# Second attention: where the mask, the ranks' comparison and the read of the flags stand in VectorE's queue

## The chip, the cores and the metric

The kernel runs on one core of a Trainium2 chip. The metric is the time of one launch on the device in microseconds (us); smaller is better. The core has TensorE (matmuls), VectorE, ScalarE, GpSimd and the queues that issue DMAs, each with an instruction stream of its own; they meet at semaphores. In the rows PE is TensorE, DVE is VectorE, ACT is ScalarE, POOL is GpSimd.

## The reference, cut to what matters

Two layers of attention and experts run one after the other on x of shape (4, 1024, 128). The change lies in the second attention alone, in which each query keeps only the 307 highest of its 1024 scores:

```python
# _L1_attn_ref: B, T, D, H = 4, 1024, 128, 16 here; hd = 8
topk = max(1, int(Tx * 0.3))                       # 307
scores = jnp.einsum('bhid,bhjd->bhij', q, k) * scale
topk_scores, indices = jax.lax.top_k(scores, topk)
masked = jnp.full_like(scores, -jnp.inf)
masked = masked.at[bi, hi, ti, indices].set(topk_scores)
attn = jax.nn.softmax(masked, axis=-1)
out = jnp.einsum('bhij,bhjd->bhid', attn, v)
```

## The kernel before, in words

`attention1` (lines 985 to 1502) works on 512 tiles: 4 batches x 16 heads x 8 blocks of 128 queries, each tile 128 queries by 1024 keys. No tile is sorted. For each the kernel finds the 307th highest score from a guess and a correction, and stages of this search are spread over the engines with a lag in tiles. The program is unrolled: `tile_slots` calls a function `slot(it, h)` for h = 0, 1, 2, ... on each engine, and in slot h each engine does its stage for tile h minus that stage's lag. So the order of each engine's work is written out by hand in `slot`.

- TensorE, slot h: the scores `S` of tile h (line 1134, two products of 512 columns); a third of the product of probabilities and values for a quad of tiles (line 1150, in three of four slots); in every eighth slot (`closes`) the column sums of the `signals` of eight tiles, `FL` (line 1162); in one of four slots the transpose of the output (line 1169); then `ST`, the scores of tile h - 16 with keys on the partitions, and the mask added through a product with the identity (lines 1181, 1182, sixteen products).
- ScalarE, slot h: Sign of `S` minus a first threshold, counted (line 1198); Sign of `z` of tile h - 1, counted (line 1205); in even slots the mask of tile h - 15 (line 1213, on ScalarE because that tile is odd); exp of `ST` (line 1220); in one of four slots a copy of the output (line 1226).
- GpSimd, slot h: from ScalarE's first count the corrected threshold `thr1` (lines 1259, 1261); in one of four slots the final cut (1266), a flag (1268) and its steep form (1271), and in another the split of four maxima; from the second count `side`, then `near` = `side` minus `z` on 128 x 1024 values as integers (line 1285), and `rank` (1288).
- VectorE, slot h: `z` = `S` + `thr1` of tile h - 1 with its maximum (line 1417); the sort of the candidates of tile h - 4 to the 16 best (`sort_first` line 1395, `sort_rest` line 1403, `sort_last` line 1411); the four searches `top(0)` to `top(3)`, each the 8 highest of a quarter of `near` of tile h - 3 (line 1381). Beside these, by slot: h % 4 == 0 the choice of the edge among the 16 best for a quad (lines 1428 comparison of ranks `hits`, 1434 `picked`, 1438 `edge`, 1443 and 1444 `signals`); odd h the mask of tile h - 15 (line 1462); h % 4 == 2 the reciprocal of the denominators and the scaled context `ctx` (lines 1473, 1480); and in every second of those, h % 8 == 6, the closing slot: VectorE sums the flags in `FL` (line 1489, `seen`, `flag_sum`), loads the sum into a register and branches (lines 1495, 1496). A sum above zero means that a tile of the eight needs the slow path `general`.

`OT` and `FL` lie in the same bank of PSUM. Before the change TensorE waits (`normed`) until VectorE has scaled the context out of `OT` before it writes `FL`; the idle copy (line 1494) is a copy of one value that nobody reads.

## Time and profile before

| what | value |
| --- | --- |
| median of 3 runs | 3462.47 us (3461.37 to 3471.24) |
| the profiled execution, its own time | 3468.05 us |
| its span | 3466.3 us, mean granted clock 0.802 |
| VectorE busy | 2752.5 us (79%), 8588 instructions |
| TensorE busy | 2636.8 us (76%) |
| ScalarE busy | 2452.2 us (71%) |
| GpSimd busy | 2014.0 us (58%) |
| second attention, first to last `z` | 1021.2 to 3006.9 us |

The profile is of one execution. Busy times are sums over the whole span; the second attention is the long middle of it, and only rows of that stretch tell what bounds it. "Idle before" is the time that an engine did nothing in front of an instruction, with what ended it; "issue" means that nothing the profile shows ended it.

### The profile page before, as it was taken

The page shows a single profiled execution, that of the slowest core. Times are in us where ns is not written, and L with a number is a line of the kernel's source. Part 1 is how long each engine was busy: PE and PEld are TensorE (multiplying, and loading weights), DVE is VectorE, ACT ScalarE, POOL GpSimd, SP SyncE. Part 2 cuts the span into 40 slices and gives each one's busy share as a digit, 9 for nine tenths or more (in the row PEclk, how much of TensorE's full clock was granted, in tenths as well). Part 3 has the DMA queues.
Part 4 walks back from the last instruction along what each step waited for, and adds up shares of the span by engine and source line. Part 5 has one row for each costly group of instructions (what it writes and reads, how often), then busy time and mean ns, then how long its engine had stood idle before and what let it go on. Part 6 is the DMA issues. An engine that isn't in the chain of part 4 may idle for free. (4 is left out here: it accounts for less than half of the span.)

```text
span 3466.3 us, 74747 instructions
## 1 busy us (share of the span) xinstructions
PE 2636.8 (76%) x23705; PEld 1489.1 (43%) x23705; DVE 2752.5 (79%) x8588; ACT 2452.2 (71%) x4051; POOL 2014.0 (58%) x4543
## 2 busy tenths in 40 slices
PE   3699999677645777777777777776777777758999
PEld 2233333233423454444455444443444444544444
DVE  5788888326439999999999999998999999844444
ACT  2266666433128999999999999997999999822221
POOL 3134333410228888888888888886888888640000
PEclk8699999888656777777777777776777777768999
DMA  5211221010230101101100110110110110010000
GB/s 149 89 52 49 53 56 30 12 34 16 75 56 2 15 5 17 18 2 17 17 9 11 17 16 4 17 17 2 17 18 2 17 17 2 2 32 3 7 7 9
DMA packets 115266, 85.88 MB, mean 25 GB/s; under 512 B 58154, under 2 KB 97340, under 8 KB 114876
## 3 DMA queue, kind: packets, MB, share of 16 engines
q1 hardware_dynamic: 106331, 75.20, 10.1%
q0 software_dynamic: 8192, 4.79, 0.9%
q8 instruction: 185, 3.03, 0.4%
q14 instruction: 206, 1.68, 0.2%
q10 hardware_dynamic: 352, 1.18, 0.1%
HBM read 54.25 MB, written 19.40 MB: 21 GB/s over the span
## 5 line engine op out<-in xcount | busy, mean ns | idle before, releaser
L1285 POOL TENSOR_TENSOR a_near<-a_side,a_z 128x1024 int32<-128x1024 int32 x512 | 969.0, 1892 | 42.6
L1181 PE MATMUL a_ST<-a_qs,a_ks 75*128 75x128 bf16 x4096 | 696.7, 259 | 336.0 <-ACT a_eT L1220 205.5
L1381 DVE MAX8 a_cand<-a_near 128x8 f32<-128x256 f32 x2048 | 750.8, 410 | 0.0
L1417 DVE TENSOR_SCALAR_CACHE_REDUCE a_z<-a_S,a_thr 128x1024 f32<-128x1024 f32 x512 | 649.1, 1268 | 81.2 <-issue 54.2
L1181 PEld LDWEIGHTS a_ST<-a_qs,a_ks 75*128 75x128 bf16 x4096 | 479.0, 118 | 526.1 <-issue 519.9
L1205 ACT ACTIVATE a_signs<-a_z,a_tiny 128x1024 bf16<-128x1024 f32 x512 | 589.3, 1151 | 76.7 <-DVE a_z L1417 70.3
L1198 ACT ACTIVATE a_signs<-a_S,search 128x1024 bf16<-128x1024 f32 x512 | 572.2, 1118 | 24.1 <-PE a_S L1134 24.0
L1220 ACT ACTIVATE a_eT<-a_ST 128x1024 f32<-128x1024 f32 x512 | 521.0, 1018 | 32.0 <-PE a_ST L1182 31.2
L776 ACT ACTIVATE a_eT<-a_ST 128x512 f32<-128x512 f32 (+3 forms) x768 | 329.3, 489 | 210.0 <-PE a_ST L761 148.9
L1134 PE MATMUL a_S<-a_ks,a_qs 72*128 72x512 bf16 x1024 | 409.1, 490 | 80.6 <-DVE a_z L1417 55.7
L880 DVE TENSOR_REDUCE a_mx<-a_S 128x1 f32<-128x512 f32 (+3 forms) x768 | 381.7, 548 | 77.9 <-PE a_S L748 68.2
L1150 PE MATMUL a_O<-a_eT,a_v 128*9 128x128 f32 x8192 | 408.0, 347 | 1.4 <-ACT wq L1226 1.4
L1182 PE MATMUL a_ST<-ident_b,a_mask 128*128 128x128 bf16 x2048 | 359.7, 264 | 0.0
L1182 PE MATMUL a_ST<-a_minus_b,a_mask 128*128 128x128 bf16 x2048 | 345.7, 257 | 0.0
L1150 PEld LDWEIGHTS a_O<-a_eT,a_v 128*9 128x9 f32 x8192 | 223.0, 108 | 262.5 <-issue 222.9
L1213 ACT ACTIVATE a_mask<-a_z,a_cut_steep 128x1024 bf16<-128x1024 f32 x256 | 291.8, 1140 | 0.0
L1462 DVE TENSOR_SCALAR a_mask<-a_z,a_cut 128x1024 bf16<-128x1024 f32 x256 | 245.4, 959 | 3.4 <-PE a_ST L1182 3.4
L1182 PEld LDWEIGHTS a_ST<-ident_b,a_mask 128*128 128x128 bf16 x2048 | 246.7, 120 | 0.0
L1182 PEld LDWEIGHTS a_ST<-a_minus_b,a_mask 128*128 128x128 bf16 x2048 | 239.2, 117 | 0.0
L2002 ACT ACTIVATE f_gate<-f_G 128x512 f32<-128x512 f32 x112 | 66.9, 597 | 243.5 <-PE f_W L1968 196.1
L758 PE MATMUL a_ST<-a_qs,a_ks 128*128 128x512 bf16 (+3 forms) x768 | 205.8, 330 | 3.2 <-ACT a_eT L776 2.9
L455 POOL TENSOR_TENSOR p_kres<-p_kf,p_kp 128x512 f32<-128x512 f32 x16 | 21.5, 1341 | 276.9 <-ACT p_kp L429 276.9
(342 smaller groups left out, 4636.5 us busy)
## 6 DMA issues: line engine op xcount, KB each, us to landing
a_qs<-q_parts SPq DMA_DIRECT2D x174, 64.0 KB
a_ks<-k_parts SPq DMA_DIRECT2D x174, 64.0 KB
a_qs<-a_flip SPq DMA_DIRECT2D x512, 0.8 KB
q_parts<-p_qp SPq DMA_DIRECT2D x48, 128.0 KB, 1.8
k_parts<-p_kp SPq DMA_DIRECT2D x48, 128.0 KB, 1.8
a_qs<-q_parts SPq DMA_DIRECT2D x60, 96.0 KB
a_ks<-k_parts SPq DMA_DIRECT2D x60, 96.0 KB
f_w<-L_ffn_W SPq DMA_DIRECT2D x16, 256.0 KB, 2.9
```

The costliest lines, as they stand in the source:

```text
L776: act.activation(eT[:, gi % 4, p % G, 0:hi - lo], ST[p % TURNED][:, 0:hi - lo], ACT.Exp, scale=SCALE0).then_inc(e_done, 1)
L880: dve.tensor_reduce(mx[:, lo // CW, col(j) // P + i:col(j) // P + i + 1], S[j][:, 0:hi - lo], AX, ALU.max).then_inc(max_s, 1)
L1134: mm = pe.matmul(S[h % 2][:, lo:lo + CW], qs[0:STACK, tile(h):tile(h) + P], ks[0:STACK, base(h) + lo:base(h) + lo + CW], start=True, stop= ...
L1150: mm = pe.matmul(O[32 * j:32 * j + HD + 1, :], v[:, h0 // PAIR % 2, kb, j * (HD + 1):(j + 1) * (HD + 1)], eT[:, h0 % RING + j, kb * P:(kb ...
L1181: pe.matmul(ST[:, block_of], ks[:, base(hl) + kb * P:base(hl) + (kb + 1) * P], qs[:, tile(hl):tile(hl) + P], start=True, stop=False)
L1182: mm = pe.matmul(ST[:, block_of], mask[:, hl % MASKS, block_of], minus_b[:, :] if hl % 2 else k.ident_b[:, :], start=False, stop=True)
L1198: act.activation(signs[:, 0, :], S[h % 2][:, :], ACT.Sign, bias=first[:, bass.ds(n, 1)], accum_out=sgn[0][:, one]).then_inc(cnt1, 1)
L1205: act.activation(signs[:, 1, :], z[:, hl, :], ACT.Sign, bias=tiny[:, :], accum_out=sgn[1][:, hl:hl + 1]).then_inc(cnt2, 1)
L1220: act.activation(eT[:, hl % RING, :], ST[:, :], ACT.Exp, scale=SCALE1).then_inc(e_done, 1)
L1285: pool.tensor_tensor(near[:, hl % NEARS, :].bitcast(I32), side[:, one].bitcast(I32).broadcast_to([P, SEQ]), z[:, hl % H, :].bitcast(I32), ...
L1381: mm = dve.max(found[:, 8 * g:8 * g + 8], near[:, h2 % NEARS, g * SW:(g + 1) * SW])
L1417: dve.tensor_scalar(z[:, h1 % H, :], S[h1 % 2][:, :], thr1[:, h1 % H:h1 % H + 1], None, ALU.add, ALU.max, accum_out=zmax[:, h1 % H:h1 % H ...
```

## The change

On VectorE, in the slots h % 4 == 0 the comparison of the ranks moves behind the second search (with the last sort now behind the first search), the product and the sum of the picks behind the third and the fourth, and the two flags' comparisons follow with no search between. In odd slots the mask moves from behind the replacement to between `top(2)` and `top(3)`. In closing slots the sum of the flags moves from between `top(2)` and `top(3)` to in front of the reciprocal, and the idle copy is left out. On TensorE the flags' product no longer waits for `normed`.

```diff
--- before.py
+++ after.py
@@ -1157,8 +1157,6 @@
                     pe.wait_ge(far_s, 2 * group + 2)
                     if not (isinstance(it, int) and group == 0):
                         pe.wait_ge(checked, group)
-                    shown = quad(it, h, NL) + 2
-                    pe.wait_ge(normed, min(max(shown, 1), QUADS + 1) if isinstance(it, int) else shown)
                     pe.matmul(FL, k.ones[:, 0:1], signals[:, h0:h0 + 8, :].rearrange("p j c -> p (j c)"), start=True, stop=True).then_inc(flag_p, 1)
                 if lagged(it, h, OTL, UN, TOTAL) is not None and ends(h, OTL):
                     q = quad(it, h, OTL)
@@ -1422,29 +1420,28 @@
                     first_sorted()
                     sort_rest()
                     near_made()
+                    top(0)
+                    rest_made()
+                    sort_last()
+                    top(1)
                     if has4 is not None:
                         dve.wait_ge(rank_s, l4 + 1)
                         dve.wait_ge(sort_s, SORTS * l4 + SORTS)
                         dve.tensor_tensor(hits[:, :, :], odd2[:, :].rearrange("p (o r) -> p o r", o=1).broadcast_to([P, 4, WINDOW]),
                                           wide(rank[:, four], WINDOW), ALU.is_equal).then_inc(choice_s, 1)
-                    rest_made()
-                    sort_last()
+                    top(2)
                     if has4 is not None:
                         dve.wait_ge(choice_s, 2 * q4 + 1)
                         dve.tensor_tensor(picked[:, :, :], hits[:, :, :], best[:, ring4, :], ALU.mult).then_inc(choice_s, 1)
-                    top(0)
+                    top(3)
                     if has4 is not None:
                         dve.wait_ge(choice_s, 2 * q4 + 2)
                         dve.tensor_reduce(edge[:, four], picked[:, :, :], AX, ALU.add).then_inc(edge_s, 1)
-                    top(1)
-                    if has4 is not None:
                         open_ends = cand[:, ring4, :].rearrange("p j (g r) -> p j g r", r=8)[:, :, :, 7]
                         dve.wait_ge(edge_s, q4 + 1)
                         dve.tensor_tensor(signals[:, four, WINDOW:FAR], open_ends, wide(edge[:, four], SEGS), ALU.is_gt)
                         dve.tensor_tensor(signals[:, four, 0:WINDOW], best[:, ring4, :], wide(edge[:, four], WINDOW),
                                           ALU.is_equal).then_inc(bad_s, 1)
-                    top(2)
-                    top(3)
                 elif h % 2:
                     if lagged(it, h, FLIPL, UN, TOTAL) is not None and ends(h, FLIPL):
                         q, ring = quad(it, h, FLIPL), ((h - FLIPL) // 4) % 2
@@ -1455,17 +1452,23 @@
                     first_sorted()
                     sort_rest()
                     near_made()
+                    top(0)
+                    rest_made()
+                    sort_last()
+                    top(1)
+                    top(2)
                     if lagged(it, h, PICK, UN, TOTAL) is not None:
                         dve.wait_ge(cut_s, it * QU + (h - PICK) // 4 + 1)
                         if not (isinstance(it, int) and lp < MASKS):
                             dve.wait_ge(turned, lp - (MASKS - 1))
                         dve.tensor_scalar(mask[:, hp % MASKS, :], z[:, hp % H, :], cut[:, hp % H:hp % H + 1], AWAY,
                                           ALU.is_lt, ALU.mult).then_inc(mask_s, 1)
-                    rest_made()
-                    sort_last()
-                    for g in range(SEGS):
-                        top(g)
+                    top(3)
                 else:
+                    if closes(it, h):
+                        group = groups(it, h)
+                        dve.wait_ge(flag_p, group + 1)
+                        dve.tensor_scalar(seen[:, :], FL, 1.0, None, ALU.mult, ALU.add, accum_out=flag_sum[:, :]).then_inc(flag_v, 1)
                     q, hn = quad(it, h, NL), here(h, NL + 3) % H
                     norm = lagged(it, h, NL, UN, TOTAL) is not None
                     if norm:
@@ -1483,15 +1486,10 @@
                     sort_last()
                     top(1)
                     top(2)
-                    if closes(it, h):
-                        group = groups(it, h)
-                        dve.wait_ge(flag_p, group + 1)
-                        dve.tensor_scalar(seen[:, :], FL, 1.0, None, ALU.mult, ALU.add, accum_out=flag_sum[:, :]).then_inc(flag_v, 1)
                     top(3)
                     if closes(it, h):
 
                         dve.wait_ge(flag_v, group + 1)
-                        dve.tensor_copy(idle[:, 2 * (h % H) + 1:2 * (h % H) + 2], half[0:1, :])
                         total = dve.value_load(flag_sum[0:1, 0:1].bitcast(I32), min_val=0, max_val=2 ** 31 - 1)
                         with dve.If(total > 0):
                             dve.tensor_reduce(flags[:, :], FL.rearrange("p (j c) -> p j c", c=VIEWS), AX, ALU.add)
```

The instruction lists of VectorE in a slot with h % 4 == 0 (`a_hits` is the comparison, `a_cand` a search, `a_best` a sort). Before:

```order
L1403 MATCH_REPLACE a_rest<-a_best,a_cand 128x32 [waits a1_sort]
L1428 TENSOR_TENSOR a_hits<-a_odd,a_rank 128x64 [waits a1_sort,a1_rank,a1_near]
L1411 MAX a_best<-a_rest 128x8 [waits a1_sort]
L1434 TENSOR_TENSOR a_picked<-a_hits,a_best 128x64 [waits a1_choice]
L1381 MAX a_cand<-a_near 128x8
L1438 TENSOR_REDUCE a_edge<-a_picked 128x4 [waits a1_choice]
L1381 MAX a_cand<-a_near 128x8
L1443 TENSOR_TENSOR a_signals<-a_cand,a_edge 128x4x4 [waits a1_edge]
L1444 TENSOR_TENSOR a_signals<-a_best,a_edge 128x4x16
L1381 MAX a_cand<-a_near 128x8 x2
```

and now:

```order
L1401 MATCH_REPLACE a_rest<-a_best,a_cand 128x32 [waits a1_sort]
L1379 MAX a_cand<-a_near 128x8 [waits a1_near]
L1409 MAX a_best<-a_rest 128x8 [waits a1_sort]
L1379 MAX a_cand<-a_near 128x8
L1430 TENSOR_TENSOR a_hits<-a_odd,a_rank 128x64 [waits a1_sort,a1_rank]
L1379 MAX a_cand<-a_near 128x8
L1435 TENSOR_TENSOR a_picked<-a_hits,a_best 128x64 [waits a1_choice]
L1379 MAX a_cand<-a_near 128x8
L1439 TENSOR_REDUCE a_edge<-a_picked 128x4 [waits a1_choice]
L1442 TENSOR_TENSOR a_signals<-a_cand,a_edge 128x4x4 [waits a1_edge]
L1443 TENSOR_TENSOR a_signals<-a_best,a_edge 128x4x16
```

The comparison and the product are each one or two searches later, and the edge's sum stands next to the comparison that waits for it; line numbers are two lower.

VectorE in an odd slot. Before:

```order
L1454 STREAM_TRANSPOSE a_flip<-a_parts 128x32 [waits a1_top_in,a1_part]
L1403 MATCH_REPLACE a_rest<-a_best,a_cand 128x32 [waits a1_sort]
L1462 TENSOR_SCALAR a_mask<-a_z,a_cut 128x1024 [waits a1_turned,a1_cut,a1_near]
L1411 MAX a_best<-a_rest 128x8 [waits a1_sort]
L1381 MAX a_cand<-a_near 128x8 x4
L1417 TENSOR_SCALAR a_z,a_zmax<-a_S,a_thr 128x1024 [waits a1_mask_a,a1_thr1]
```

and now:

```order
L1451 STREAM_TRANSPOSE a_flip<-a_parts 128x32 [waits a1_top_in,a1_part]
L1401 MATCH_REPLACE a_rest<-a_best,a_cand 128x32 [waits a1_sort]
L1379 MAX a_cand<-a_near 128x8 [waits a1_near]
L1409 MAX a_best<-a_rest 128x8 [waits a1_sort]
L1379 MAX a_cand<-a_near 128x8 x2
L1464 TENSOR_SCALAR a_mask<-a_z,a_cut 128x1024 [waits a1_turned,a1_cut]
L1379 MAX a_cand<-a_near 128x8
L1415 TENSOR_SCALAR a_z,a_zmax<-a_S,a_thr 128x1024 [waits a1_mask_a,a1_thr1]
```

The mask stands behind three of the four searches; the wait for `near` is at the first search.

VectorE in a closing slot. Before:

```order
L1417 TENSOR_SCALAR a_z,a_zmax<-a_S,a_thr 128x1024 [waits a1_mask_a,a1_thr1]
L1395 MAX a_best<-a_cand 128x8 [waits a1_top]
L1473 RECIPROCAL a_rden<-a_OT 128x4 [waits a1_o_turned]
L1403 MATCH_REPLACE a_rest<-a_best,a_cand 128x32 [waits a1_sort]
L1480 TENSOR_TENSOR ctx<-a_OT,a_rden 128x32 [waits a1_rden,a1_near]
L1381 MAX a_cand<-a_near 128x8
L1411 MAX a_best<-a_rest 128x8 [waits a1_sort]
L1381 MAX a_cand<-a_near 128x8 x2
L1489 TENSOR_SCALAR a_seen,a_flag_sum<-a_OT 1x176 [waits a1_flag_p]
L1381 MAX a_cand<-a_near 128x8
L1494 COPY a_idle<-a_half 1x1 [waits a1_flag_v]
L1495 TENSOR_LOAD a_flag_sum
L1495 ISA x2
```

and now:

```order
L1415 TENSOR_SCALAR a_z,a_zmax<-a_S,a_thr 128x1024 [waits a1_mask_a,a1_thr1]
L1393 MAX a_best<-a_cand 128x8 [waits a1_top]
L1471 TENSOR_SCALAR a_seen,a_flag_sum<-a_OT 1x176 [waits a1_flag_p]
L1476 RECIPROCAL a_rden<-a_OT 128x4 [waits a1_o_turned]
L1401 MATCH_REPLACE a_rest<-a_best,a_cand 128x32 [waits a1_sort]
L1483 TENSOR_TENSOR ctx<-a_OT,a_rden 128x32 [waits a1_rden,a1_near]
L1379 MAX a_cand<-a_near 128x8
L1409 MAX a_best<-a_rest 128x8 [waits a1_sort]
L1379 MAX a_cand<-a_near 128x8 x3
L1493 TENSOR_LOAD a_flag_sum [waits a1_flag_v]
L1493 ISA x2
```

The flags' sum, with its wait for TensorE's product (`a1_flag_p`), has moved ahead of the reciprocal, and the register load follows the last search.

TensorE around the flags' product. Before:

```order
L1150 MATMUL a_O<-a_eT,a_v 9x128 x12
L1162 MATMUL a_OT<-a_signals,ones 1x176 [waits a1_checked,a1_normed,a1_far,a1_bad]
L1181 MATMUL a_ST<-a_qs,a_ks 128x128 [waits a1_exp,a1_mask]
```

and now:

```order
L1150 MATMUL a_O<-a_eT,a_v 9x128 x12
L1160 MATMUL a_OT<-a_signals,ones 1x176 [waits a1_checked,a1_far,a1_bad]
L1179 MATMUL a_ST<-a_qs,a_ks 128x128 [waits a1_exp,a1_mask]
```

The wait `a1_normed` is gone; the place is the same.

## Rows read from the trace of the kernel before

**Rows 1.** Windows view: window, length, busy us per engine, clock, DMA share, GB/s
```profile
1400.00:1700.00 300.00, 225.11 (x2717) 145.41 (x2720) 290.28 (x1010) 292.99 (x449) 259.33 (x630) 0.78 0.10 14
```

**Rows 2.** Waits, 1100 to 3000 us: engine and line, waited for, us, times, longest
```profile
PE a_OT L1162 <- DVE ctx L1480: 133.5, 60, 3.1
...
DVE a_z L1417 <- issue: 52.0, 61, 5.1
ACT a_signs L1205 <- DVE a_z L1417: 51.9, 99, 19.1
...
ACT a_eT L1220 <- PE a_ST L1182: 15.2, 34, 0.9
```

**Rows 3.** Line 1417 (ns min/median/max, first and last start), and its VectorE timeline
```profile
L1417 DVE TENSOR_SCALAR_CACHE_REDUCE a_z<-a_S,a_thr x512: 1256/1266/1285, 1021.2 to 3006.9; 128x1024 f32<-128x1024 f32 x171
...
2015.63 1.26 DVE L1417 TENSOR_SCALAR_CACHE_REDUCE a_z<-a_S,a_thr 128x1024 f32<-128x1024 f32 x1
...
2019.84 1.26 DVE L1417 TENSOR_SCALAR_CACHE_REDUCE a_z<-a_S,a_thr 128x1024 f32<-128x1024 f32 x1
```

**Rows 4.** ScalarE timeline: start, us, engine, line, out<-in, count
```profile
2001.55 1.10 ACT L1198 ACTIVATE a_signs<-a_S,search 128x1024 bf16<-128x1024 f32 x1
...
2016.38 1.13 ACT L1198 ACTIVATE a_signs<-a_S,search 128x1024 bf16<-128x1024 f32 x1
```

**Rows 5.** Lines 1462 and 1428: duration ns min/median/max, first and last start
```profile
L1462 DVE TENSOR_SCALAR a_mask<-a_z,a_cut x256: 741/843/1575, 1069.4 to 3037.1; 128x1024 bf16<-128x1024 f32 x128
...
L1428 DVE TENSOR_TENSOR a_hits<-a_odd,a_rank x128: 212/608/905, 1044.5 to 3017.4; 128x64 f32<-128x64 f32 x128
```

**Rows 6.** VectorE's groups, 1500 to 2500 us: busy us, mean ns, idle before
```profile
L1462 DVE TENSOR_SCALAR a_mask<-a_z,a_cut 128x1024 bf16<-128x1024 f32 x127 | 121.3, 955 | 0.0
...
L1428 DVE TENSOR_TENSOR a_hits<-a_odd,a_rank 128x64 f32<-128x64 f32 x64 | 33.8, 529 | 0.0
```

**Rows 7.** VectorE timeline, two masks
```profile
2017.21 1.29 DVE L1462 TENSOR_SCALAR a_mask<-a_z,a_cut 128x1024 bf16<-128x1024 f32 x1
...
2025.54 0.74 DVE L1462 TENSOR_SCALAR a_mask<-a_z,a_cut 128x1024 bf16<-128x1024 f32 x1
```

**Rows 8.** GpSimd timeline around the same two masks
```profile
2016.06 1.89 POOL L1285 TENSOR_TENSOR a_near<-a_side,a_z 128x1024 int32<-128x1024 int32 x1
2017.91 0.64 POOL L1288 TENSOR_TENSOR a_rank<-a_sgn,a_shifted 128x1 f32<-128x1 f32 x1
...
2018.77 0.19 POOL L1261 TENSOR_TENSOR a_thr<-a_scaled,search 128x1 f32<-128x1 f32 x1
...
2019.08 0.25 POOL L1268 TENSOR_SCALAR a_signals<-a_rank 128x4 f32<-128x4 f32 x1
...
2022.91 1.89 POOL L1285 TENSOR_TENSOR a_near<-a_side,a_z 128x1024 int32<-128x1024 int32 x1
```

**Rows 9.** VectorE timeline, end of a closing slot [idle before <-releaser]
```profile
2022.84 0.41 DVE L1381 MAX8 a_cand<-a_near 128x8 f32<-128x256 f32 x1
2023.18 0.12 DVE L1494 COPY a_idle<-a_half 1x1 f32<-1x1 f32 x1
2023.93 1.28 DVE L1417 TENSOR_SCALAR_CACHE_REDUCE a_z<-a_S,a_thr 128x1024 f32<-128x1024 f32 x1 [0.63 <-issue]
```

**Rows 10.** VectorE timeline, a sort and the replacement that needs it
```profile
2008.82 0.20 DVE L1395 MAX8 a_best<-a_cand 128x8 f32<-128x32 f32 x1
2009.05 0.09 DVE L1403 MATCH_VALUE_LOAD a_rest<-a_best,a_cand 128x8 f32 x1
```

**Rows 11.** TensorE timeline: S products at both speeds, and the flags' product
```profile
2013.93 1.06 PE L1134 MATMUL a_S<-a_ks,a_qs 72*128 72x512 bf16 x2
...
2017.59 0.59 PE L1134 MATMUL a_S<-a_ks,a_qs 72*128 72x512 bf16 x2
...
2021.74 0.46 PE L1162 MATMUL a_OT<-a_signals,ones 128*1 128x176 f32 x2 [2.79 <-DVE ctx L1480]
```

## The prediction

> **What bounds the kernel now.** I read the busy shares by stretch first, then the waits of each engine over the steady part of the second attention, then its timelines for one group of eight tiles. In the stretch from 1400 to 1700 us VectorE is busy 290.28 of 300 us, ScalarE 292.99, GpSimd 259.33 and TensorE 225.11 at a mean granted clock of 0.78 [rows 1]. Two engines are nearly full, so the shares alone don't name the bound. The waits do: between 1100 and 3000 us VectorE never waits for another engine in front of its first instruction of a tile. It has only 52.0 us marked "issue", 61 times, once per group of eight tiles. ScalarE waits 51.9 us for VectorE's `z` (19.1 of that is one single wait, the one group of tiles that goes through the slow branch) and 15.2 us for TensorE's `ST` [rows 2]. So VectorE sets the pace, with ScalarE close behind.
>
> The stage runs 512 tiles. Their `z` instructions start between 1021.2 and 3006.9 us [rows 3], 1985.7 us; without the one slow branch some 1967 us, or 30.8 us per eight tiles (64 such groups). ScalarE alone would need, for four tiles, the distance between two of its first Sign instructions in a part where it hardly waits: 2016.38 - 2001.55 = 14.83 us [rows 4], about 14.78 without the 0.05 to 0.08 us it does wait there. That is 29.6 us for eight, 1892 us for the stage. **The most that any relief of VectorE can give is therefore 1967 - 1892 = 75 us**; beyond that ScalarE is the bound.
>
> **The change, part by part.**
>
> *The mask (line 1462, 256 times, odd slots).* It isn't removed, it moves from right behind the sort's replacement to between the third and the fourth search. What that buys is read from its duration: 741 ns at least, 1575 at most [rows 5], a mean of 955 [rows 6]. The timeline says why. The mask that began at 2017.21 took 1.29 us (to 18.50); GpSimd's `near` subtraction (line 1285) ran from 2016.06 to 17.95, and the mask ended 0.55 us behind it. The mask at 2025.54 took 0.74; `near` had started at 2022.91, so it was over at 24.80 [rows 7, 8]. The two don't run together: the mask waits for `near` to end and then runs. Right behind it GpSimd's own small `rank` took 0.64 us, where its neighbour of the same size (`thr1`, 2018.77) took 0.19, so the loss goes both ways [rows 8]. In the new order the mask comes later by three searches and the last sort, 3 x 0.34 us (the distance of two starts in [rows 9]) and about 0.1 for the sort, 1.1 us: 2.7 us behind its tile's `z` instead of 1.58 (2017.21 - 2015.63, [rows 3, 7]). `near` ended 2.3 us behind `z` in that slot, so the mask is clear of it. Searches and sorts stand in its place, and the mask's neighbours there, searches of 0.41 us, are not stretched anywhere in these rows. Bounds: nothing gained if it meets the next `near` as often as it met this one, all of it if never. 256 x (0.955 - 0.741) = **55 us**. I take all of it, being nearest to the free row.
>
> *The ranks' comparison (line 1428, 128 times).* Same case: 212 ns at least, 905 at most [rows 5], mean 529 [rows 6]. It moves behind two searches and the last sort, some 0.8 us, and lands at about 2.4 us behind `z`. 128 x (0.529 - 0.212) = **41 us**. The product moves one search down too and is no longer held by the comparison. On the other side, the sum of the picks (1438) and the flags that need it (1443) now stand together with no search between. What a dependent neighbour costs: an instruction that waits for nothing starts 0.07 us before the end of the one in front (2022.84 + 0.41 against 2023.18, [rows 9]); the replacement, which needs the sort in front of it, starts 0.03 us behind that one's end (2008.82 + 0.20 against 2009.05, [rows 10]). The difference is 0.10 us, 128 x 0.10 = **-13 us**. Lower end nothing, if the step's own write is short.
>
> *The count of the flags (line 1489, 64 times) and the idle copy.* The count itself stays, moved to the head of the slot. The idle copy goes, and what stood behind it: `z` started 0.75 us behind the copy's start (2023.93 - 2023.18), with 0.63 idle, marked issue [rows 9]. That is the register load of the sum and the branch. If this delay runs from the start of the instruction in front, it now runs from the last search, and `z` comes 0.34 us earlier; if from its end, 0.12 us earlier. 64 x 0.34 = 22 us or 64 x 0.12 = 8 us; I take 15, the middle, since no row tells the two apart.
>
> *The new wait at the head of the slot.* VectorE now stands at the flags' sum before the reciprocal, and behind it are queued the scaling, four searches and the next `z`, on which ScalarE and TensorE wait. TensorE's product (line 1162) loses its wait for the scaled context: it stood 2.79 us, until 2021.74 [rows 11], 133.5 us in all over 60 of them [rows 2]. Without that wait it could have begun at 18.95, but for GpSimd's last flag, written 2019.08 to 19.33 [rows 8]; it takes 0.46 at half speed, so the sum is there at about 19.8. VectorE wants it about 1.3 us into a slot that began at 2019.84 [rows 3], at 21.1. Cover: 1.3 us. If VectorE runs ahead by that much, or TensorE works the part in front at its low clock (two S products took 1.06 us instead of 0.59, [rows 11]), the cover is gone and the wait is up to 0.9 us by estimate, 64 x 0.9 = 58 us on VectorE at worst. I take zero, since a wait that arises only when VectorE is ahead costs only the lead. The turn behind that product starts 2.3 us sooner, which takes away part of the 15.2 us that ScalarE waits for `ST`.
>
> **Sum.** VectorE alone: 55 + 41 - 13 + 15 = 98 us less, 1967 - 98 = 1869. ScalarE alone: 1892. So ScalarE becomes the bound, and 23 us of the 98 bring nothing. Of the cap of 75 I keep the waits for TensorE (15) and some 5 for slots in which VectorE still comes late, because mask slots of ScalarE are 1 us longer than the others while VectorE's are even: **gain 55 us**. Against the profiled execution of 3468.05 us (span 3466.3) that is 3413; the median of the runs, 3462.47, lies 5.6 below it, so I forecast 3407.5.
>
> The first thing to weigh against this: the mask and GpSimd exclude each other in both directions [rows 7, 8], so a mask that starts first holds up whatever GpSimd does next. The Trainium skill states this as a rule (SBUF — State Buffer, "Who interferes with whom": the one that issues first has the shared port pair for its whole instruction, the other blocks fully), and the trace agrees, 0.64 against 0.19 us. By that rule the cost doesn't vanish but changes sides; it is the second rival.
>
> **Rivals.**
> 1. *The wait moves* (chance 0.20). The flags' sum comes late at TensorE's low clock, or the bias of the next `z` (`thr1`) does, and VectorE waits where before it never did. For it: VectorE will be faster than ScalarE and so run ahead into these waits. Against it: 1.3 us of cover now. If the whole 58 us stay on VectorE, it needs 1869 + 58 = 1927, which is a gain of 40, or 25 if the 15 us of waits for TensorE come on top; the middle is 33: 3430.
> 2. *The lock falls on GpSimd's path to `z`: slower* (0.06). The later mask runs from 2.7 to 3.4 us behind `z`; GpSimd's scaling and sum that make `thr1` stood in the profile just behind the `rank` that was held, i.e. from 2.9 us on [rows 8]. If they are caught each time and VectorE waits for them, it loses 0.55 us (0.741 less the start-up) at 256 masks, 141 us, against a gain of 98: 43 us slower, 3505; it decides from 0.42 us per mask ((98 + 10)/256). Against it: GpSimd's part comes forward by the 0.45 us for which `rank` no longer waits, and the next `z` starts 0.9 us behind the end of `thr1` now (2018.96 against 2019.84, [rows 3, 8]).
> 3. *TensorE takes over* (0.08). It is busy 75% at a clock of 0.78; if the clock fell to 0.58, the same work would fill the time (0.75 x 0.78/0.58 = 1.0) and the gain would be gone: 3460. For it: a mean of 0.78 between 2.4 GHz (1) and 1.2 GHz (0.5) already means 44% of the time at the low level. Against it: taking idle time out of TensorE has no reason in these rows to lower its clock.
> That the change does nothing is excluded for the orders: the instruction lists show both moves.
>
> **Numbers.** Forecast case 0.66, gain 45 to 70 us. About 0.3% (10 us) is what a measurement of this kernel can tell from no change. Faster: 0.66 + 0.20 and a little of rival 3, 0.87; same 0.07; slower 0.06. The range reaches from the cap (3462.5 - 75 = 3388) to rival 1 with a smaller gain (25 us, 3437).
>
> **What would show it.** The mask's mean down from 955 to about 750 ns and the comparison's from 529 to about 220; ScalarE's waits for `z` down from 52 to under 10 us (beside the slow branch) and ScalarE busy over 99% of the stage; the tiles 29.7 to 29.9 us per eight; the gap behind the last search of a closing slot 0.4 to 0.6 us. Wrong: waits of VectorE's count for TensorE, of `z` for `thr1`, a mask mean still over 850 ns, or ScalarE's waits for `ST` grown beyond 30 us.

## The result, and the profile after

The changed kernel takes 3386.43 us (median of 4 runs, 3382.49 to 3389.14) against 3464.64 for the kernel before, timed beside it: a ratio of 0.977, 95% interval 0.975 to 0.979. That is 78 us less, where 55 were forecast, and 1 to 2 us below the low end of the range.

The page of the profiled execution (3382.49 us, span 3380.8): busy time of each engine, and the groups of the second attention that matter:

```profile
PE 2580.7 (76%) x23705; PEld 1478.1 (44%) x23705; DVE 2683.7 (79%) x8524; ACT 2426.5 (72%) x4051; POOL 2026.2 (60%) x4543
...
L1415 DVE TENSOR_SCALAR_CACHE_REDUCE a_z<-a_S,a_thr 128x1024 f32<-128x1024 f32 x512 | 653.8, 1277 | 63.3 <-POOL a_thr L1259 57.2
L1203 ACT ACTIVATE a_signs<-a_z,a_tiny 128x1024 bf16<-128x1024 f32 x512 | 648.7, 1267 | 34.8 <-DVE a_z L1415 34.8
...
L1218 ACT ACTIVATE a_eT<-a_ST 128x1024 f32<-128x1024 f32 x512 | 577.7, 1128 | 13.2 <-PE a_ST L1180 13.1
```

ScalarE's lines 1203 and 1218 (1205 and 1220 before) show longer means than before, 1267 and 1128 ns against 1151 and 1018. Their starts are no further apart: behind a Sign of `z` the next record starts 1.04 us later in both kernels, behind an exp 0.90 us (medians from 1100 to 2900 us). So the records overlap more than before, and starts, not durations, tell ScalarE's pace here.

The windows view of the stretch of [rows 1] (window, length, busy us of PE, PEld, DVE, ACT, POOL, clock, DMA):

```profile
1400.00:1700.00 300.00, 228.01 (x2827) 152.30 (x2815) 292.84 (x1033) 300.00 (x468) 271.19 (x652) 0.77 0.11 16
```

ScalarE is busy 300.00 of 300 us, where it was 292.99. The waits, 1100 to 2920 us:

```profile
DVE a_z L1415 <- POOL a_thr L1259: 29.0, 174, 0.2
...
ACT a_signs L1203 <- DVE a_z L1415: 20.0, 2, 19.8
...
DVE a_z L1415 <- issue: 5.7, 1, 5.7
```

These answer to [rows 2]. ScalarE waits twice, 19.8 of 20.0 us in the one slow branch; the 15.2 us for `ST` are gone altogether. TensorE no longer stands for the scaled context. VectorE now waits for `thr1`, 174 times by at most 0.2 us, 29.0 us in all. It is the engine ahead.

The lines moved (ns min/median/max), with what ended the idle time in front of the flags' sum, first the mask, then the comparison, then the sum, from the views of their lines:

```profile
L1464 DVE TENSOR_SCALAR a_mask<-a_z,a_cut x256: 732/736/1460, 1069.3 to 2951.2; 128x1024 bf16<-128x1024 f32 x128
```

```profile
L1430 DVE TENSOR_TENSOR a_hits<-a_odd,a_rank x128: 204/207/656, 1045.4 to 2934.4; 128x64 f32<-128x64 f32 x128
```

```profile
L1471 DVE TENSOR_SCALAR_CACHE_REDUCE a_seen<-a_OT x64: 309/310/331, 1064.4 to 2940.7; 1x176 f32<-1x176 f32 x64
...
  PE a_OT L1160: 5.0, 2
```

The mask's median went from 843 to 736 ns and the comparison's from 608 to 207 [rows 5]. The new wait at the flags' sum cost 5.0 us in the whole execution.

The `z` instruction, against [rows 3]:

```profile
L1415 DVE TENSOR_SCALAR_CACHE_REDUCE a_z<-a_S,a_thr x512: 1255/1280/1286, 1021.7 to 2924.0; 128x1024 f32<-128x1024 f32 x171
```

Its first and last start are 1902.3 us apart, 83.4 less than before; the whole span is 85.5 us shorter, so some 2 us lie outside this stretch. ScalarE's timeline over four tiles, against [rows 4]:

```profile
2002.78 1.30 ACT L1196 ACTIVATE a_signs<-a_S,search 128x1024 bf16<-128x1024 f32 x1
...
2017.66 1.20 ACT L1196 ACTIVATE a_signs<-a_S,search 128x1024 bf16<-128x1024 f32 x1
```

14.88 us lie between these two, of which some 0.15 is a late exp; the median distances of all its tiles in the stage are 3.12, 4.16, 3.28 and 4.16 us for tiles that follow each other, 14.72 for four. VectorE's timeline, a mask and a closing slot:

```profile
2001.12 0.73 DVE L1464 TENSOR_SCALAR a_mask<-a_z,a_cut 128x1024 bf16<-128x1024 f32 x1
...
2009.78 1.28 DVE L1415 TENSOR_SCALAR_CACHE_REDUCE a_z<-a_S,a_thr 128x1024 f32<-128x1024 f32 x1 [0.15 <-POOL a_thr L1259]
...
2011.09 0.31 DVE L1471 TENSOR_SCALAR_CACHE_REDUCE a_seen<-a_OT 1x176 f32<-1x176 f32 x1
...
2012.15 1.06 DVE L1379 MAX8 a_cand<-a_near 128x8 f32<-128x256 f32 x3
2013.16 1.28 DVE L1415 TENSOR_SCALAR_CACHE_REDUCE a_z<-a_S,a_thr 128x1024 f32<-128x1024 f32 x1
```

The mask at 2001.12 takes 0.73 us. In the closing slot the flags' sum stands in front; three searches start at 2012.15, and `z` starts at 2013.16, 1.01 us later. That is three searches at 0.34 us: the register load and the branch between them cost VectorE nothing. Before, they cost 0.63 us of idle time [rows 9], and 0.93 in every other group.

GpSimd's timeline at the same mask:

```profile
1998.80 1.89 POOL L1283 TENSOR_TENSOR a_near<-a_side,a_z 128x1024 int32<-128x1024 int32 x1
...
2001.21 0.69 POOL L1259 TENSOR_TENSOR a_thr<-a_scaled,search 128x1 f32<-128x1 f32 x1
...
2004.79 0.19 POOL L1259 TENSOR_TENSOR a_thr<-a_scaled,search 128x1 f32<-128x1 f32 x1
...
2008.60 0.73 POOL L1286 TENSOR_TENSOR a_rank<-a_sgn,a_shifted 128x1 f32<-128x1 f32 x1
```

`thr1` at 2001.21 took 0.69 us instead of 0.19: the mask had begun at 2001.12. `near`, which began at 1998.80, was over by then. This is no exception. From 1100 to 2900 us there are 240 masks, and beside 238 of them one of GpSimd's instructions on 128 x 1 values takes over 0.5 us: `thr1` 118 times, `rank` 116, another one 4 times. So the lock falls on GpSimd's path to `z` in nearly every slot with a mask. Whether `z` feels it depends on which one is held. Where it was `thr1` itself, the next `z` started on time (2002.11, 0.34 us behind the search in front). Where it was `rank`, as at 2008.60, the `thr1` behind it came late, and `z` at 2009.78 stood 0.15 us for it.

### The profile page after: what moved, and what is told of

It reads as the page before. It is cut to its first block and busy times, and to the rows that moved or that the text cites. A ratio compares the mean times of both kernels' runs of the same rounds, so it can differ in the third digit from the quotient of the medians.

```text
span 3380.8 us, 74612 instructions
## 1 busy us (share of the span) xinstructions
PE 2580.7 (76%) x23705; PEld 1478.1 (44%) x23705; DVE 2683.7 (79%) x8524; ACT 2426.5 (72%) x4051; POOL 2026.2 (60%) x4543
## 5 line engine op out<-in xcount | busy, mean ns | idle before, releaser
L1379 DVE MAX8 a_cand<-a_near 128x8 f32<-128x256 f32 x2048 | 804.2, 414 | 0.4 <-issue 0.4
L1203 ACT ACTIVATE a_signs<-a_z,a_tiny 128x1024 bf16<-128x1024 f32 x512 | 648.7, 1267 | 34.8 <-DVE a_z L1415 34.8
L1196 ACT ACTIVATE a_signs<-a_S,search 128x1024 bf16<-128x1024 f32 x512 | 629.0, 1228 | 24.3 <-PE a_S L1134 24.3
L1218 ACT ACTIVATE a_eT<-a_ST 128x1024 f32<-128x1024 f32 x512 | 577.7, 1128 | 13.2 <-PE a_ST L1180 13.1
L880 DVE TENSOR_REDUCE a_mx<-a_S 128x1 f32<-128x512 f32 (+3 forms) x768 | 381.1, 547 | 77.3 <-PE a_S L748 67.7
L1150 PE MATMUL a_O<-a_eT,a_v 128*9 128x128 f32 x8192 | 373.9, 325 | 1.4 <-ACT wq L1224 1.4
L1211 ACT ACTIVATE a_mask<-a_z,a_cut_steep 128x1024 bf16<-128x1024 f32 x256 | 322.0, 1258 | 0.0
L1150 PEld LDWEIGHTS a_O<-a_eT,a_v 128*9 128x9 f32 x8192 | 212.4, 103 | 242.9 <-issue 212.0
L1464 DVE TENSOR_SCALAR a_mask<-a_z,a_cut 128x1024 bf16<-128x1024 f32 x256 | 199.2, 778 | 3.4 <-PE a_ST L1180 3.4
```

Source lines behind the costliest of these rows:

```text
L880: dve.tensor_reduce(mx[:, lo // CW, col(j) // P + i:col(j) // P + i + 1], S[j][:, 0:hi - lo], AX, ALU.max).then_inc(max_s, 1)
L1150: mm = pe.matmul(O[32 * j:32 * j + HD + 1, :], v[:, h0 // PAIR % 2, kb, j * (HD + 1):(j + 1) * (HD + 1)], eT[:, h0 % RING + j, kb * P:(kb ...
L1196: act.activation(signs[:, 0, :], S[h % 2][:, :], ACT.Sign, bias=first[:, bass.ds(n, 1)], accum_out=sgn[0][:, one]).then_inc(cnt1, 1)
L1203: act.activation(signs[:, 1, :], z[:, hl, :], ACT.Sign, bias=tiny[:, :], accum_out=sgn[1][:, hl:hl + 1]).then_inc(cnt2, 1)
L1218: act.activation(eT[:, hl % RING, :], ST[:, :], ACT.Exp, scale=SCALE1).then_inc(e_done, 1)
L1379: mm = dve.max(found[:, 8 * g:8 * g + 8], near[:, h2 % NEARS, g * SW:(g + 1) * SW])
```

## The experiments

All ratios are to the kernel before, timed beside each on the same chip; its medians lay between 3463.5 and 3465.2 us.

### The parts alone

**Mask alone.** `top(0)`, the last sort, `top(1)` and `top(2)` in front of the mask in odd slots, all else as before.

```diff
+                    top(0)
+                    rest_made()
+                    sort_last()
+                    top(1)
+                    top(2)
                     if lagged(it, h, PICK, UN, TOTAL) is not None:
...
-                    rest_made()
-                    sort_last()
-                    for g in range(SEGS):
-                        top(g)
+                    top(3)
```

> The kernel before with the mask alone moved between the third and the fourth search. Theory A (VectorE paces the kernel before, and the lock with GpSimd's near stretches the mask): the mask's mean falls from 955 to about 750 ns and the whole kernel gains 256 x 0.2 = 45 to 55 us. Theory B (the gain of the whole change came from TensorE no longer standing at the flags' product): mask shorter, but the time falls by less than 20 us. Theory C (the lock changes sides): mask shorter, VectorE waits for thr1, gain under 20 us.

Measured: 3452.9 us, ratio 0.996 (0.995 to 0.998), 11 us. **Ranks' comparison alone**, the block of slots with h % 4 == 0 as in the changed kernel, all else as before:

```diff
                     near_made()
+                    top(0)
+                    rest_made()
+                    sort_last()
+                    top(1)
                     if has4 is not None:
...
-                    rest_made()
-                    sort_last()
+                    top(2)
...
```

> The kernel before with the ranks' comparison and what follows it alone moved. Theory A: the comparison falls from 529 to about 210 ns, and the kernel gains 41 - 13 = 28 us. Theory B: no more than 5 us.

Measured: 3461.5 us, ratio 0.9995 (0.9986 to 1.0005), nothing. **Flags' part alone** (the old place of the sum, behind `top(2)`, is among what is left out of the diff):

```diff
-                    shown = quad(it, h, NL) + 2
-                    pe.wait_ge(normed, min(max(shown, 1), QUADS + 1) if isinstance(it, int) else shown)
...
                 else:
+                    if closes(it, h):
+                        group = groups(it, h)
+                        dve.wait_ge(flag_p, group + 1)
+                        dve.tensor_scalar(seen[:, :], FL, 1.0, None, ALU.mult, ALU.add, accum_out=flag_sum[:, :]).then_inc(flag_v, 1)
...
-                        dve.tensor_copy(idle[:, 2 * (h % H) + 1:2 * (h % H) + 2], half[0:1, :])
```

> The kernel before with the flags' part alone: sum at the head of the closing slot, TensorE's wait for the scaled context out, idle copy out; mask and comparison as before. In the changed kernel the gap in front of z in a closing slot is gone, not only shorter. If the register load's delay counts from the flags' sum (about 1.0 us behind it in the kernel before), it is hidden here too and VectorE gains 64 x 0.75 to 1.04 us plus nothing else: 50 to 65 us. By the step of the prediction it would be 8 to 22 us. Theory B: 60 us or more, with ScalarE's waits for ST gone.

Measured: 3450.6 us, ratio 0.996 (0.995 to 0.998), 13 us. The three parts alone make 26 us, the whole 78. VectorE's groups of the two locked instructions between 1500 and 2500 us (busy us, mean ns, idle before) say where the rest went, for mask alone, comparison alone and flags alone:

```profile
L1467 DVE TENSOR_SCALAR a_mask<-a_z,a_cut 128x1024 bf16<-128x1024 f32 x128 | 94.0, 735 | 0.0
...
L1428 DVE TENSOR_TENSOR a_hits<-a_odd,a_rank 128x64 f32<-128x64 f32 x64 | 45.8, 716 | 0.0
```

```profile
L1461 DVE TENSOR_SCALAR a_mask<-a_z,a_cut 128x1024 bf16<-128x1024 f32 x128 | 135.4, 1058 | 0.0
...
L1432 DVE TENSOR_TENSOR a_hits<-a_odd,a_rank 128x64 f32<-128x64 f32 x64 | 13.2, 206 | 0.0
```

```profile
L1460 DVE TENSOR_SCALAR a_mask<-a_z,a_cut 128x1024 bf16<-128x1024 f32 x129 | 133.5, 1035 | 0.0
...
L1426 DVE TENSOR_TENSOR a_hits<-a_odd,a_rank 128x64 f32<-128x64 f32 x64 | 44.7, 699 | 0.0
```

Read against [rows 6], 955 and 529 ns: each relief is there in full on its own line (735 ns; 206 ns), and **the other exposed instruction has become longer**. With the mask moved, the comparison waits 716 ns; with the comparison moved, the mask takes 1058; with the gap in front of `z` gone, 1035 and 699. What holds these instructions is not a fixed price. They wait until GpSimd's `near` is over, and a VectorE that comes earlier waits longer.

How much of each relief that explains can be added up. The sums are of VectorE's start-to-start times over 44 groups in the middle of the stage, scaled to 64:

| run | relief | given back | left | time measured |
| --- | --- | --- | --- | --- |
| mask alone | mask 59 | comparison 22, starts of `z` late 23 | 14 | 11 |
| comparison alone | comparison 44 | mask 25, edge and flags 20 | 0 | 2 |
| flags alone | gap and idle copy 55 | mask 20, comparison 20 | 15 | 13 |

So in the run with the comparison alone nearly half of what was lost is not the lock: VectorE spends 20 us more at the sum of the picks and the flags behind it, which now stand next to each other. In the run with the mask alone there is a second sink besides the comparison, `z` itself. The waits of this run from 1100 to 2900 us, then VectorE and GpSimd at the end of a slot with h % 8 == 2:

```profile
ACT a_eT L1220 <- PE a_ST L1182: 41.9, 67, 0.9
...
DVE a_z L1417 <- POOL a_thr L1261: 6.0, 31, 0.2
```

```profile
2036.09 1.06 DVE L1381 MAX8 a_cand<-a_near 128x8 f32<-128x256 f32 x3
2037.34 1.28 DVE L1417 TENSOR_SCALAR_CACHE_REDUCE a_z<-a_S,a_thr 128x1024 f32<-128x1024 f32 x1 [0.20 <-POOL a_thr L1261]
```

```profile
2034.86 1.89 POOL L1285 TENSOR_TENSOR a_near<-a_side,a_z 128x1024 int32<-128x1024 int32 x1
...
2037.12 0.19 POOL L1261 TENSOR_TENSOR a_thr<-a_scaled,search 128x1 f32<-128x1 f32 x1
```

`z` starts 1.25 us behind the three searches' start instead of 1.01: `thr1` stands behind `near` in GpSimd's order, and a VectorE that runs ahead meets it there too. The waits view counts only what lies behind the end of the last search (6.0 us), so it shows a fraction of this. ScalarE waits 41.9 us for `ST` in this run, where it was 15.2.

Theory A (the terms add) falls with all three runs. Theory B (TensorE's stand is all) fits the first two, since it asked for less than 20 and at most 5 us there; it falls with the third, which was to bring 60 us and brought 13. Theory C (VectorE waits for `thr1` instead) is true in part for the mask alone: its gain under 20 us and these waits came as it said.

### Two parts at a time

**Mask and comparison, flags as before:**

> Mask and comparison moved, the flags' part as before. Theory A: the sum of the two single runs, 70 to 83 us, but no more than the 82 us at which ScalarE becomes the bound; ScalarE still waits a little for ST, because TensorE still stands at the flags' product. Theory B: less than half of the 78 us of the whole change.

Measured: 3418.6 us, ratio 0.987 (0.986 to 0.989), 45 us: more than the 13 of the single runs together, less than the 70 to 83 of theory A. The waits of this run show what is left:

```profile
PE a_OT L1162 <- DVE ctx L1481: 84.4, 59, 2.2
...
DVE a_z L1417 <- issue: 50.6, 59, 5.1
```

**Mask and flags, comparison as before:**

> Mask moved and the flags' part changed, the ranks' comparison left in its old place. The single runs gave 11, 2 and 13 us, mask and comparison together 45, the whole 78. Theory D (give-back): whatever VectorE gains it spends by arriving earlier at the instruction that is still exposed to near's lock; here the comparison alone, 128 times, so its mean stays near 700 ns and the gain is between 40 and 60 us. Theory A (terms simply add, up to ScalarE's floor): 11 + 13 = 24 us.

Measured: 3388.0 us, ratio 0.978 (0.976 to 0.980), 77 us: the whole gain, with the comparison still in its old place, and more than the 40 to 60 expected. **Comparison and flags, mask as before:**

> Comparison moved and the flags' part changed, the mask left in its old place. Theory D: the mask, 256 times exposed, takes back nearly all that the other two give: its mean rises to 1.1 to 1.2 us and the gain stays under 25 us. Theory A by the lock's own price (41 us less 13, and the gap of 58 us): 70 us or more.

Measured: 3440.9 us, ratio 0.993 (0.991 to 0.995), 24 us. The same two groups of both, first with the comparison left exposed, then with the mask:

```profile
L1465 DVE TENSOR_SCALAR a_mask<-a_z,a_cut 128x1024 bf16<-128x1024 f32 x133 | 97.8, 736 | 0.0
...
L1426 DVE TENSOR_TENSOR a_hits<-a_odd,a_rank 128x64 f32<-128x64 f32 x66 | 47.4, 717 | 0.0
```

```profile
L1459 DVE TENSOR_SCALAR a_mask<-a_z,a_cut 128x1024 bf16<-128x1024 f32 x128 | 153.6, 1200 | 0.4 <-POOL a_near L1283 0.2 <-issue 0.2
...
L1430 DVE TENSOR_TENSOR a_hits<-a_odd,a_rank 128x64 f32<-128x64 f32 x65 | 13.4, 206 | 0.0
```

Here is the give-back at its clearest. The mask, exposed in four of eight slots, rises to 1200 ns and takes 256 x (1.200 - 0.736) = 119 us more than a free one, where it took 56 in the kernel before. The comparison, exposed in two, also rises (717 ns, 128 x 0.51 = 65 us), but that costs nothing any more: ScalarE is already the bound, and VectorE has that much to spare. So the move of the comparison brings no time in the changed kernel (3388.0 against 3386.4), though its line shows 41 us less.

### How far the mask must move

**Mask behind the first search only**, 0.44 us later than before:

```diff
                     near_made()
+                    top(0)
+                    rest_made()
+                    sort_last()
                     if lagged(it, h, PICK, UN, TOTAL) is not None:
...
-                    rest_made()
-                    sort_last()
-                    for g in range(SEGS):
-                        top(g)
+                    top(1)
+                    top(2)
+                    top(3)
```

> The kernel before with the mask moved behind the first search and the last sort only, 0.44 us later instead of 1.1. If the mask is held until near ends (1.8 to 2.3 us behind z), a mask that comes at 2.0 is still caught in the slots in which near ends late: mean near 800 to 850 ns, gain 25 to 45 us, between none and the full move. If only the order of the instructions mattered (no lock), gain as with the full move or none.

Measured: 3454.3 us, ratio 0.997 (0.996 to 0.998). The mask's mean follows the distance, 955, 812, 735 ns for 0, 0.44 and 1.1 us, as a wait for the end of `near` must:

```profile
L1465 DVE TENSOR_SCALAR a_mask<-a_z,a_cut 128x1024 bf16<-128x1024 f32 x128 | 104.0, 812 | 0.0
```

The time, 9 us, is below the 25 to 45 expected, for the reason above (the comparison takes 737 ns in this run).

### The gap in front of `z`

**No idle copy**, all else before:

```diff
-                        dve.tensor_copy(idle[:, 2 * (h % H) + 1:2 * (h % H) + 2], half[0:1, :])
```

> The kernel before without the idle copy, all else the same. If the load's delay counts from the flags' sum (1.02 us in the trace before), z starts where it did: gain 0 to 3 us and a gap longer by 0.1 us. If it counts from the instruction in front of the load: gain 8 us (from its end) or 22 us (from its start), as the prediction had it.

Measured: ratio 1.000 (0.999 to 1.001). **Idle copy put back** in front of the load of the changed kernel (the same line with +):

> The changed kernel with the idle copy put back in front of the register load. ScalarE is the bound, so nothing: within 3 us. If VectorE still were the bound, +6 to +10 us, or +40 and more if the copy brings the gap in front of z back.

Measured: 3384.9 us, ratio 0.977 (0.976 to 0.979), no difference from the changed kernel's. The idle copy is free in either. **Load made to wait for the last search:**

```diff
                         dve.wait_ge(flag_v, group + 1)
+                        if has2 is not None:
+                            dve.wait_ge(top_s, l2 + 1)
```

> The changed kernel with the register load made to wait for the last search, so that the gap in front of z in the closing slot comes back (0.6 to 1.0 us, 64 times) while TensorE still doesn't stand at the flags' product. Tells what of the 33 us between mask-and-ranks (3418.6) and the whole change (3386.4) is the gap and what is TensorE's stand. If the gap: about 3410 to 3420. If TensorE's stand (ScalarE then waits for ST): 3386 to 3395, since the 47 us of copies cost nothing.

Measured: 3455.0 us, ratio 0.997 (0.996 to 0.998), against 3410 to 3420 expected: one wait of a register load, 64 times, costs 69 us of the 78. Its VectorE timeline in two closing slots that follow each other, and what ended the idle time in front of `z` in the view of line 1415 (us, times), with who waited for `z`:

```profile
2014.61 1.06 DVE L1379 MAX8 a_cand<-a_near 128x8 f32<-128x256 f32 x3
2016.75 1.28 DVE L1415 TENSOR_SCALAR_CACHE_REDUCE a_z<-a_S,a_thr 128x1024 f32<-128x1024 f32 x1 [1.08 <-issue]
...
2044.74 1.06 DVE L1379 MAX8 a_cand<-a_near 128x8 f32<-128x256 f32 x3
2047.18 1.28 DVE L1415 TENSOR_SCALAR_CACHE_REDUCE a_z<-a_S,a_thr 128x1024 f32<-128x1024 f32 x1 [1.37 <-issue]
```

```profile
  issue: 80.6, 62
...
  ACT a_signs L1203: 77.3, 120
```

The gap is 1.08 us behind the last search's end in one group and 1.37 in the next, and ScalarE waits for `z` 77.3 us in the whole run. Since the only thing changed is which semaphore the load waits for, the delay runs from that semaphore: load and branch take 1.1 or 1.4 us behind their wait, in turns. In the kernel before it ran from the end of the flags' sum, whose last part is this record:

```profile
2022.84 0.07 DVE L1489 DVE_READ_ACCUMULATOR a_seen<-a_OT 1x1 f32 x1
```

It ended at 2022.91; `z` started 1.02 us later [rows 9], 0.63 of it idle, and 1.31 us later in every other group. With the sum at the slot's head it is over long before the searches are. The gap of this run is not the old one: the closing slot is 4.80 us long here (median from `z` to `z`) against 4.39 in the kernel before, since the delay begins 0.34 us later, at the end of the last search.

**TensorE's stand alone.** The wait for the scaled context put back, behind the flags' product:

```diff
                     pe.matmul(FL, k.ones[:, 0:1], signals[:, h0:h0 + 8, :].rearrange("p j c -> p (j c)"), start=True, stop=True).then_inc(flag_p, 1)
+                    shown = quad(it, h, NL) + 2
+                    pe.wait_ge(normed, min(max(shown, 1), QUADS + 1) if isinstance(it, int) else shown)
```

> The changed kernel with TensorE's wait for the scaled context put back, but behind the flags' product, so that VectorE gets the sum early and TensorE alone stands, some 1.5 to 2 us, 64 times. If TensorE's stand made a part of the gain: +5 to +35 us, with ScalarE waiting for ST. If the gain of the flags' part is the gap in front of z alone: within 3 us.

Measured: 3390.0 us, ratio 0.978 (0.976 to 0.980), inside the changed kernel's interval. Its waits:

```profile
PE a_ST L1181 <- DVE ctx L1485: 67.3, 59, 1.2
...
ACT a_signs L1205 <- DVE a_z L1417: 19.9, 2, 19.7
```

TensorE stands 67 us and ScalarE doesn't notice. So of the 32 us between mask-and-comparison and the whole change, TensorE's stand made no more than 4 here (3390.0 less 3386.4); the gap in front of `z` is what is left.

### How much VectorE has to spare

**One copy of one value in every slot** of the changed kernel, then **two in every slot**, then **eight in the closing slot** behind the last sort:

```diff
+                dve.tensor_copy(idle[:, 2 * (h % H):2 * (h % H) + 1], half[0:1, :])
                 listed()
                 sort_first()
```

> The changed kernel with one copy of one value more on VectorE in each of the 534 slots, about 0.09 us each, 47 us of VectorE work. If VectorE has slack behind ScalarE, as ScalarE's busy share of 100% says, the time rises by less than that: slack by the sum of the free-running slots is 0.6 to 0.9 us per eight tiles, 40 to 60 us, so +0 to +10 us. If VectorE still paces the kernel, +40 to +47 us.

> The changed kernel with two small copies in every slot, 2 x 0.09 us x 534 = 95 us of VectorE work. Sets the slack: one copy cost nothing. With a slack of about 50 us in all, +40 to +50 us; with more, less.

> The changed kernel with eight small copies, about 0.75 us, in the closing slot alone, behind the last sort: the same VectorE work as one copy in each slot, which cost nothing (3386.5). Theory of the lead: VectorE can't bank a lead, since thr1 holds it back, so 0.75 us in one slot comes out partly as a late z: +10 to +40 us. Theory of the sum (only the work per eight tiles counts, as the prediction reckoned): +0 to +3 us.

Measured: 3386.5 us (ratio 0.978), 3388.6 us (0.978, 0.976 to 0.980) and 3390.2 us (0.979, 0.977 to 0.980). The copies were cheaper than expected; the eight of the last run took 0.48 us from start to start:

```profile
2015.97 0.55 DVE L1489 COPY a_idle<-a_half 1x1 f32<-1x1 f32 x8
2016.45 1.06 DVE L1379 MAX8 a_cand<-a_near 128x8 f32<-128x256 f32 x3
```

In the other two, one copy delays the sort behind it by 0.07 and two by 0.12 us, so some 35 and 60 us of VectorE work went in for 0 and 2 us; 0.48 us in one slot (31 us in all) cost 4, within the intervals. That doesn't separate the lead theory (extra work in one slot comes out as a late `z`) from the sum (only the work per eight tiles counts); the copies were too short for it. The load's gap is 1.4 us of start-to-start distance in one slot (4.80 against 3.38).

### Is ScalarE the bound now

**The copy of the output out of PSUM moved from ScalarE to VectorE**, first between the edge's sum and the flags' comparison (3.4 us behind `z`), then right behind the first sort (the second is shown):

```diff
-                if lagged(it, h, OCL, UN, TOTAL) is not None and ends(h, OCL):
-                    q = quad(it, h, OCL)
...
-                    act.activation(oT[((h - OCL) // 4) % 2][:, :], O[:, :], ACT.Copy).then_inc(oc, 1)
...
                 sort_first()
                 if h % 4 == 0:
+                    if lagged(it, h, OCL + 1, UN, TOTAL) is not None and ends(h, OCL + 1):
+                        qo = quad(it, h, OCL + 1)
+                        dve.wait_ge(pv, qo + 2)
+                        if not (isinstance(it, int) and qo < 2):
+                            dve.wait_ge(ot, qo)
+                        dve.tensor_copy(oT[((h - OCL - 1) // 4) % 2][:, :], O[:, :]).then_inc(oc, 1)
```

> The changed kernel with the copy of the output out of PSUM (128 times, 0.16 us of ScalarE each) moved from ScalarE to VectorE, between the edge's sum and the comparison that waits for it. If ScalarE is the only bound and VectorE has slack: 128 x 0.16 = 20 us less, 3364 to 3370. If VectorE or GpSimd's thr1 is the bound right behind: 3380 to 3388. If the copy meets TensorE late: slower.

Measured: 3432.1 us, ratio 0.991 (0.989 to 0.994), 46 us slower than the changed kernel. TensorE stood for the late copy:

```profile
PE a_O L1150 <- DVE wq L1439: 61.3, 58, 1.9
```

> As the run before with the output's copy on VectorE, but the copy stands right behind the first sort, about 1.3 us behind z instead of 3.4, so that TensorE (which stood 61 + 19 us for it) gets it in time. If ScalarE alone is the bound of the changed kernel: 20 us less than it, 3364 to 3370. If VectorE's path through thr1 is the bound right behind ScalarE: 3378 to 3390. If TensorE still stands for the copy: 3400 or more.

Measured: **3367.6 us, ratio 0.972 (0.970 to 0.974)**, faster than both kernels and 19 us faster than the changed one; 128 copies at 0.16 us are 20. ScalarE is still busy for the whole of its window:

```profile
1400.00:1700.00 300.00, 227.08 (x2837) 153.20 (x2835) 294.89 (x1066) 300.00 (x454) 269.95 (x657) 0.77 0.11 16
```

```profile
2008.45 1.26 DVE L1409 TENSOR_SCALAR_CACHE_REDUCE a_z<-a_S,a_thr 128x1024 f32<-128x1024 f32 x1
...
2009.75 0.27 DVE L1419 COPY wq<-a_O 128x128 f32<-128x128 f32 x1
```

The median distances of ScalarE's tiles now add up to 14.56 us for four instead of 14.72, so the time fell with its pace. That shows both: ScalarE is the bound of the changed kernel, and what is taken from it comes out in full as long as nobody is made to wait.

## Why the prediction came out as it did

The step that failed is the last one, from ScalarE's cap to the forecast: the cap of 75 us was too low, and the 20 us held back from it (15 for ScalarE's waits for `ST`, 5 for late slots) did not arise. The terms on VectorE's side were wrong too, but their sum lay above the cap in the forecast and in the run, so they didn't move the number.

- **What bounds the kernel before: right**, with an addition. VectorE set the pace. But a part of its own "work" was waiting, inside the durations of two instructions, for GpSimd's `near`. The waits view showed none of it.
- **Mask and comparison: the mechanism right, the sum wrong.** The lines changed as forecast (735 to 778 ns, 207 ns). The step "256 x 0.214 = 55 and 128 x 0.317 = 41, to be added" failed: alone they brought 11 us and nothing, since much of what was saved at one was waited off at the other and at `z`. Each is worth its line only when no exposed instruction remains behind it, or when another engine is the bound. The price of the dependent neighbours was set at 13 us; by the starts it was some 0.15 us, 128 times, 19 us.
- **The gap in front of `z`: the term on VectorE that was mis-sized most.** It was put at 15 us, taking the delay to run from the instruction in front of the load. It runs from the semaphore the load waits for, and it vanished: `z` starts on the searches' own beat. In VectorE's distances from `z` to `z` the closing slot fell from 4.39 to 3.38 us, some 64 us in all. A gap put back, 0.4 us longer than the old one, cost 69 us.
- **The wait at the flags' sum: right**, 5.0 us in all, and so was giving no time to TensorE's stand.
- **ScalarE as the new bound: right, its level not.** The cap of 75 us stood on one stretch of 14.83 us less 0.05. The stretch held more small waits than that; the median distances give 14.72 for four tiles, 1884 us for 512 and a cap of 83. The stage without its slow branch took 1902.3 - 19.8 = 1882.5 us, not 1892.
- **The 20 us held back: wrong.** ScalarE's waits for `ST` went to nothing, and no slot of ScalarE's came late. With a cap of 83 and nothing held back the forecast would have been right to 1 us in the stage; with the numbers used it ended 23 us short and its range 2 us too high. The sum on VectorE has no part in that: by the estimate below its need fell to about 1824 us (64 x 28.5), where the forecast had 1869.
- **Rivals.** The first didn't happen. The second, the lock on GpSimd's path to `z`, did happen in nearly every slot with a mask, and `z` came late where `rank` was the one held: by 0.24 us in the median, in two of eight slots, not by 0.55 in four. It costs nothing while ScalarE is the bound. The Trainium skill's rule (SBUF — State Buffer, "Who interferes with whom") is that the one that issues first has the shared pair. The trace agrees in both directions, since a mask that started first held up `thr1` (0.69 us instead of 0.19). The third didn't happen: the clock was 0.77 in the same window.

What stays open: how much of VectorE's time a gap in one slot costs. Eight free-running slots of VectorE add up to about 28.5 us (the shortest median distance of each slot over all runs), ScalarE's to 29.46; with 1.4 us more VectorE would be 0.45 over, some 30 us in the stage, where the load's gap cost 69. The waits of that run from 1100 to 2900 us show two things more:

```profile
DVE a_seen L1471 <- PE a_OT L1160: 14.7, 22, 0.9
...
DVE a_z L1415 <- POOL a_thr L1259: 8.9, 58, 0.2
```

VectorE stands at the flags' sum for TensorE, which it never did there in the changed kernel. And in two slots of each group `z` starts late by `thr1`, 0.12 and 0.25 us counted from the last search, 24 us in the stage; the second of the two is one in which the mask holds `rank`. So VectorE waits in slots in which it is ahead and is late in the one behind the gap. Together these are some 40 us, which closes the sum, but no run took either away, so it is argued, not shown; why TensorE's product came late is not known. Nor was an instruction tried that does the mask's work without being held by `near`.

## What to carry to other kernels

An instruction that is stretched by a lock is a wait in disguise, and elastic: much of the time saved elsewhere on its engine is waited off there. Look at its shortest against its mean duration, and relieve all such places together or count nothing for one. A register load that a branch needs should have its value, and the semaphore it waits for, some 1.4 us ahead or more. And take the pace of the next engine from its start-to-start medians over many tiles, not from one stretch: it is the cap of the whole forecast.

## What the runs showed of the hardware that was not expected

- The register load and its branch delay VectorE only by what is left of some 1.1 or 1.4 us (in turns from group to group) behind the semaphore they wait for; with the semaphore set long before, by nothing (2012.15 to 2013.16 for three searches and the next start).
- Each late mask held up one small instruction of GpSimd that reads and writes four bytes per partition: 0.69 or 0.73 us instead of 0.19, 238 times beside 240 masks.
- A copy of one value costs VectorE 0.06 us from start to start in a row of eight, and 0.07 alone behind `z`, not its recorded 0.12 to 0.14.
- In a stretch without waits ScalarE's records grow by some 0.1 us each (1151 to 1267 ns for the Sign of `z`) with no change of pace, so its busy share reaches 100% and the mean duration of a line says nothing of its cost.
